# A decoder layer on one core: the causal mask moves from a bf16 product on TensorE to a GpSimd select on the copied scores

## The reference, cut to what matters

```python
# B = 8 sequences of S = 512 rows, D = 512, H = 16 heads of 32
x = x + self_attention(layernorm(x))            # q and k normalised per head
x = x + cross_attention(layernorm(x), ctx)      # only the 32 largest scores of a row count
x = x + ffn(layernorm(x))                       # quantised 512 -> 2048 -> 512

# in self_attention:
scores = jnp.einsum('bhqd,bhkd->bhqk', q, k) * scale
causal = jnp.tril(jnp.ones((s, s), dtype=bool))
scores = jnp.where(causal, scores, mask_value)
attn = jax.nn.softmax(scores, axis=-1)
```

## Time and profile before

| what | value |
|---|---|
| median of 3 runs | 3978.51 us (3974.26 to 3980.03) |
| the profiled execution | 3970.88 us, its span 3968.7 us |
| busy: PE, DVE | 3343.2 us (84%), 3333.4 us (84%) |
| busy: ACT, POOL | 2460.3 us (62%), 1789.4 us (45%) |
| chain that ended last, by engine | DVE 42%, PE 26%, issue 10%, POOL 10%, ACT 4% |

### The profile page before, as it was taken

One profiled execution on the slowest core, in us unless ns is written; L12 is line 12 of the kernel. 1 busy time (PEld: TensorE's weight loads), 2 busy tenths in 40 slices (PEclk: granted clock), 3 DMA queues, 4 the chain that ended last, 5 costly groups with the idle time before them and its releaser, 6 DMA issues.

```text
span 3968.7 us, 61337 instructions
## 1 busy us (share of the span) xinstructions
PE 3343.2 (84%) x18502; PEld 2462.5 (62%) x18502; DVE 3333.4 (84%) x7699; ACT 2460.3 (62%) x4921; POOL 1789.4 (45%) x2316
## 2 busy tenths in 40 slices
PE   2487799998999889998999898998899888877765
PEld 1365577766666676666666666666666666555542
DVE  4312299999999999999988999999989999999962
ACT  3344467666766677666766676667766676555533
POOL 0123234445544454545654555446544554344433
PEclk7778878888989988988988898998898898887767
DMA  8122322232222222322323222222232221211100
GB/s 276 49 54 58 102 72 70 81 83 72 69 67 82 62 63 74 91 78 62 85 73 83 66 68 70 77 66 64 78 94 78 62 70 41 62 46 35 33 22 19
DMA packets 167443, 283.04 MB, mean 71 GB/s; under 512 B 40639, under 2 KB 52939, under 8 KB 166606
## 3 DMA queue, kind: packets, MB, share of 16 engines
q1 hardware_dynamic: 160782, 275.98, 25.5%
q10 hardware_dynamic: 6336, 3.15, 0.3%
HBM read 113.27 MB, written 31.46 MB: 36 GB/s over the span
## 4 chain that ended last, share of the span: by engine, by line
DVE 42%; PE 26%; issue 10%; POOL 10%; ACT 4%; SPq 3%; DMA 1%; DVEq 0%; POOLq 0%; ACTq 0%
DVE cW L881 18%; DVE top L876 14%; PE bank L682 6%; PE bank L607 5%; PE bank L654 4%; SPq L513 3%; POOL srs L1147 3%; PE bank L593 2%; DVE smx L1017 2%; PE bank L670 2%; DVE hh L966 2%; PE bank L635 2%; POOL cS L1168 1%; DVE hmx L969 1%; POOL hh L1115 1%
## 5 line engine op out<-in xcount | busy, mean ns | idle before, releaser
L881 DVE MATCH_REPLACE8 cW<-top,cW 128x512 f32<-128x512 f32 x1536 | 1026.5, 676 | 0.0
L876 DVE MAX8 top<-cW 128x8 f32<-128x512 f32 x1536 | 981.0, 680 | 0.0
L1168 POOL TENSOR_TENSOR cS<-cS,cW 128x512 f32<-128x512 f32 x512 | 663.1, 1317 | 216.0 <-ACT cW L825 216.0
L797 ACT ACTIVATE PT<-bank 128x512 f32<-128x512 f32 (+3 forms) x1024 | 537.6, 525 | 359.1 <-PE bank L593 355.0
L607 PE MATMUL bank<-cv,PT 128*128 128x33 f32 x4096 | 600.0, 294 | 126.0 <-ACT PT L797 125.3
L607 PEld LDWEIGHTS bank<-cv,PT 128*128 128x128 f32 x4096 | 569.9, 214 | 161.9 <-ACT PT L797 155.4
L1175 POOL TENSOR_SCALAR cnb<-top 128x2 f32<-128x2 f32 x256 | 49.1, 192 | 894.1 <-DVE top L876 880.7
L607 PEld LDWEIGHTS bank<-sv,PT 128*128 128x128 f32 x2560 | 403.9, 213 | 77.7 <-ACT PT L797 54.2
L593 PE MATMUL bank<-ident,cS 128*128 128x128 f32 x2048 | 355.2, 302 | 73.4 <-POOL cS L1168 73.4
L825 ACT ACTIVATE cW<-cW,cnb 128x512 f32<-128x512 f32 x512 | 347.8, 733 | 107.9 <-DVE cW L881 107.4
L682 PE MATMUL bank<-w_group,xT 128*128 128x384 f32 x1024 | 406.3, 545 | 0.0
(11 more groups left out here) (151 smaller groups left out, 6087.0 us busy)
## 6 DMA issues: line engine op xcount, KB each, us to landing
sk_stack<-part SPq DMA_DIRECT2D x512, 64.0 KB, 2.0
sq_stack<-part SPq DMA_DIRECT2D x512, 64.0 KB, 2.0
ck_stack<-part SPq DMA_DIRECT2D x512, 64.0 KB, 2.0
cq_stack<-part SPq DMA_DIRECT2D x512, 64.0 KB, 2.0
w_group<-wa_by_group SPq DMA_DIRECT2D x32, 768.0 KB, 4.6
w_group<-wc_by_group SPq DMA_DIRECT2D x32, 768.0 KB, 4.3
feed<-in_x SPq DMA_DIRECT2D x32, 256.0 KB, 3.0
feed<-in_ctx SPq DMA_DIRECT2D x32, 256.0 KB, 3.0
```

Of the source, the lines that this page charges most:

```text
L797: act.activation(PT[k][:, 0:n], turned_ps[k][:, 0:n], ACT.Copy).then_inc(turned_read, step("turned_read", label))
L876: dve.max(top8[:, j, r, :], src[:]).then_inc(topk, step("topk", (c, r, "max", j)))
L881: dve.match_replace(cW[j][:], top8[:, j, r, :], src[:], REPLACED).then_inc(topk, step("topk", (c, r, "replace", j)))
L1168: pool.tensor_tensor(cS[m % 2][j][:], cS[m % 2][j][:], cW[j][:], ALU.subtract).then_inc(cprob, step("cprob", (m, j)))
```

## The change

The bf16 product is gone, with its two constants. In its place POOL has one `affine_select` for each pair of heads, on the diagonal blocks of both heads in `sP`, which writes -1e30 where the key is behind the query. DVE's maxima wait for a new semaphore `masked` in place of ACT's copy, and the select waits for ACT's copy of the pair's second head. In POOL's queue `causal_mask(s, 0)` stands behind `inner_quant`, `causal_mask(s, 1)` behind `rows_ln` and ahead of `x1_ln`.

```diff
@@ scores (PE)
-                                      start=True, stop=False)
-                            pe.matmul(ps[:, qt * P:(qt + 1) * P], ident16[:], mask16[:], start=False,
-                                      stop=True).then_inc(score_full, step("score_full", label))
+                                      start=True, stop=True).then_inc(score_full, step("score_full", label))
@@ self_maxima (DVE)
-                            dve.wait_ge(score_read, upto("score_read", ("self", s, 2 * half + 1)))
+                            dve.wait_ge(masked, upto("masked", (s, half)))
@@ POOL
+                    def causal_mask(s, half):
+                        if on(s):
+                            pool.wait_ge(score_read, upto("score_read", ("self", s, 2 * half + 1)))
+                            diagonal = sP[half][:, :, (s % NT) * P:(s % NT + 1) * P]
+                            pool.affine_select(out=diagonal, in_=diagonal, compare_op=ALU.is_ge, fill=MASKED, base=0,
+                                               pattern=[[0, 2], [-1, P]], channel_multiplier=1).then_inc(
+                                                   masked, step("masked", (s, half)))
...
                         inner_quant(s - 1)
+                        causal_mask(s, 0)
                         low_parts(now[3])
...
                         rows_ln(s)
+                        causal_mask(s, 1)
                         x1_ln(s)
@@ setup (POOL)
-                pool.memset(mask16[:], 0.0).then_inc(s_const, 1)
-                pool.affine_select(out=mask16[:], in_=mask16[:], compare_op=ALU.is_ge, fill=MASKED, base=0,
-                                   pattern=[[-1, P]], channel_multiplier=1).then_inc(s_const, 1)
-                pool.wait_ge(s_const, 3)
-                pool.tensor_copy(ident16[:], ident[:])
```

More of the change, by code:

```diff
@@ L43 @@
 SIGNALS = ["shared_full", "shared_read", "score_full", "score_read", "turned_full", "turned_read",
-           "smax", "sexp", "sbias", "cbias", "cexp", "topk", "so_full", "co_full", "recip", "so_norm", "co_norm",
+           "masked", "smax", "sexp", "sbias", "cbias", "cexp", "topk", "so_full", "co_full", "recip", "so_norm", "co_norm",
            "crest", "cprob", "sq_done", "rstd_done", "shat_done", "sumsq_done", "dve_rows", "pool_rows", "feed_stats",
@@ L214, in __init__ @@
             for p in range(2):
-                for name in ("smax", "sbias", "cbias"):
+                for name in ("masked", "smax", "sbias", "cbias"):
                     add(name, (n, p))
@@ L286, in decoder_layer @@
         ident = sb("ident", [P, P])
-        ident16 = sb("ident16", [P, P], BF16)
-        mask16 = sb("mask16", [P, P], BF16)
         ones16 = sb("ones16", [96, P], BF16)
@@ L301, in decoder_layer @@
         setup(nc, dict(W_attn=W_attn, b_attn=b_attn, wa_dram=wa_dram, wc_dram=wc_dram, banks=banks,
-                       ident=ident, ident16=ident16, mask16=mask16, ones16=ones16, bias16=bias16,
+                       ident=ident, ones16=ones16, bias16=bias16,
                        minus_half=minus_half, gcol=gcol, ccol=ccol, wscale=wscale, wproj=wproj, woT=woT, wgT=wgT, wuT=wuT,
@@ L368, in pipeline @@
             upto, step = C.upto, C.step
-            (shared_full, shared_read, score_full, score_read, turned_full, turned_read, smax, sexp, sbias, cbias,
+            (shared_full, shared_read, score_full, score_read, turned_full, turned_read, masked, smax, sexp, sbias, cbias,
              cexp, topk, so_full, co_full, recip, so_norm, co_norm, crest, cprob, sq_done, rstd_done, shat_done,
@@ L1227, in setup @@
     W_attn, b_attn, wa_dram, wc_dram = T["W_attn"], T["b_attn"], T["wa_dram"], T["wc_dram"]
-    banks, ident, ident16, mask16, ones16, bias16 = (T[k] for k in ("banks", "ident", "ident16", "mask16", "ones16", "bias16"))
+    banks, ident, ones16, bias16 = (T[k] for k in ("banks", "ident", "ones16", "bias16"))
     minus_half, gcol, wscale, wproj, woT = (T[k] for k in ("minus_half", "gcol", "wscale", "wproj", "woT"))
@@ L1289, in _ @@
                 pool.memset(ident[:], 0.0).then_inc(s_const, 1)
-                pool.memset(mask16[:], 0.0).then_inc(s_const, 1)
                 pool.memset(ones16[:], 1.0)
                 pool.memset(minus_half[:], -0.5)
-                pool.wait_ge(s_const, 2)
+                pool.wait_ge(s_const, 1)
                 pool.affine_select(out=ident[:], in_=ident[:], compare_op=ALU.not_equal, fill=1.0, base=0,
                                    pattern=[[-1, P]], channel_multiplier=1).then_inc(s_const, 1)
-                pool.affine_select(out=mask16[:], in_=mask16[:], compare_op=ALU.is_ge, fill=MASKED, base=0,
-                                   pattern=[[-1, P]], channel_multiplier=1).then_inc(s_const, 1)
-                pool.wait_ge(s_const, 3)
-                pool.tensor_copy(ident16[:], ident[:])
             @block.vector
@@ L1336, in _ @@
             def _(pe):
-                pe.wait_ge(s_const, 3)
+                pe.wait_ge(s_const, 2)
                 for k in range(4):
```

## The result

The changed kernel takes 4001.25 us, the median of 5 runs (3995.27 to 4005.89), against 3978.51 us for the kernel before: a ratio of 1.005, 95% interval 1.0039 to 1.0062, or +23 us. Its profiled execution took 3997.8 us.

A forecast was written before the change was run, and what follows sets the result against it. DVE was taken to bound the full pipeline, PE close behind, and a ring the filling stage. The terms 9.6 + 14.4 + 3 + 11 - 6 = +32 us gave 4010 us, 0.8% slower; 8-in-10 range 3985 to 4038 us.

The forecast's parts named there:

- eight slots like 74: Half 1 of eight head-norm slots: select behind the second subtraction, DVE's maxima 1.2 us later each, 9.6 us in all.
- six slots like 70: Half 1, select also behind the rows' layer norm: DVE stands 6.2 us, recovers 3.8; net 2.4 each, 14.4 us.
- six slots like 66: Half 1 of six slots: DVE loses 1.2 us, swallowed by its 2.27 us wait for the output projection: 0.
- the x1 chain: Six slots: select ahead of the x1 rows' layer norm, on the way to the output projection: 0.5 us each, 3 us.
- filling stage: Slots 2, 6, 10, 14, 18: bias 1.6 us and squares 1.2 us later, less 0.7 for PE; 11 us for five groups.
- TensorE: PE's starts 0.07 us closer per dropped mask, seen only where PE sets the pace: 6 us gained over seven sequences.
- Rival (a): A select is much dearer than its columns say, up to 1.25 us: +31 more, 4041 us; 12%.
- The tight first halves: Half 0 of slots 39, 55, ...: 0.73 us between POOL and DVE against 0.6 needed; no cost at 0.4 us of select.
- the three waits behind the stall: After slot 70's maxima: DVE's waits of 0.94 and 0.47 us for subtractions, 2.42 us for the SiLU, would vanish: 3.8 us.
- (b): Stalls are swallowed in the eight slots and the filling stage: within 8 us of before, about 3984 us; 15%.
- (c): PE, not DVE, sets the pace over more of the pipeline, so the kernel gets faster: 3956 us; 7%.
- (d): POOL's added reads collide with DVE's two-input product, up to 0.4 us at each of 128: 4061 us at most; 4%.

The follow-up runs named there:

- the two complementary runs: Changed kernel with the product instead of the select in half 1 of head-norm slots: 3981.89 us; and select only there, product elsewhere: 4011.04 us.
- the early place: Changed kernel with the select ahead of the subtractions in head-norm slots: 3997.86 us; the same with the select only from slot 20: 3986.82 us.
- the complement: Changed kernel with the select only in half 1 of the slots s modulo 4 = 2 and the product in the other 224 halves: 4011.04 us.

## Why the prediction was right

The forecast (slower, by stalls of DVE behind POOL's queue) holds. The time came out 9 us under it, inside the range. That the sum came so near is partly luck, since two of its terms were too small in opposite directions. Its steps, with the trace of the changed kernel against that of before, whose spans are 27 us apart (the medians 23):

| term | predicted | in the trace |
|---|---|---|
| eight slots like 74 | 8 x 1.2 = 9.6 | 8 x 1.0 = 8 |
| six slots like 70 | 6 x 2.4 = 14.4 | 6 x 3.3 = 20 |
| six slots like 66 | 0 | 1.0 each, 0.6 to 1.0 given back |
| the x1 chain | 6 x 0.5 = 3 | 6 x 0.4 = 2 |
| filling stage | 11 | 14 (the times say 11) |
| TensorE | -6 | -17, the remainder |

**The select's price**, 0.40 us from one block's 0.29 and the slope of a one-input operation, measured 0.416. Rival (a), a dear select, is out. **The slots like 74**: the mechanism is shown by the two complementary runs and by the early place, which has no stall there, and the size is that of the gap, 0.92 us: the hand-overs of 0.1 us each were a little too large (select to maxima is 0.03 us in slot 74: 1951.65 + 0.42 to 1952.10). **The slots like 66** were swallowed as argued. **The tight first halves** cost nothing.

**The slots like 70.** The step "they now start at 1826.84: DVE stands for 6.2 us ... Net 6.2 - 3.8 = 2.4 us" was right in its form, the three waits behind the stall are gone, but two sizes were off. DVE recovers 4.8 us and not 3.8: beside the three waits L962 ran in 1.06 us and not in the 1.75 of the earlier trace rows, which is 0.7 us of it. And the stall is 5.9 us where POOL's head norm is on time, as I had assumed everywhere, so 1.2 us net (slot 86 of the complement), and 7.3 us where PE's clock was low ahead of it, 3.3 us net. The second case was in none of my steps. It is all six slots in the changed kernel, 12.8 of the 20 us; the stalls that I had priced make 7.3 us, half of my 14.4.

**The filling stage.** The times give 11 us (+23 with all selects, +12 with the product in that stage), as predicted; the trace's 14 hold 3.5 us between the maxima of slots 3 and 4 that a run with the program of before has as well. The two parts of the step are there: the bias's 1.5 us in slot 2, and for the squares 1.15 us net in slots 5 and 13, with 1.2 predicted. The "- 0.7 for PE" per group is neither shown nor refuted: with the product gone the maxima of slot 21 come 326.5 us behind the first ones in one trace and, with the product in three slots of each sequence, 324.2 us in another, against 325.8 before, and programs that are the same there differ by up to 4.6 us.

**TensorE** is the term whose size failed: "12 x 0.07 = 0.8 us per sequence, 6 us over seven sequences". The starts moved by 0.08 us as read, but the stretches in which PE sets the pace give back 1.5 us per sequence (0.2, 0.6 and 0.7 us in slots modulo 16 = 15, 0 and 8), some 9 us, and slots 62 and 94 another 3.7 us each. In slot 62 it is the clock again, the window of the changed kernel:

```profile
1570.00:1583.00 13.00, 11.85 (x74) 9.57 (x73) 12.83 (x33) 8.33 (x19) 8.38 (x12) 0.85 0.23 81
```

In the same stretch of the trace of before, 1547 to 1560 us, the granted clock is 0.64. That the product's removal caused that is not shown: slots 78 and 110 of the same traces don't have it. Taken alone the removal brought only 6 us, since the clock of the slots like 70 took 11.8 back (five of six, 1.9 to 3.3 us each). On top of the selects it brought 17: there three of the six had the low clock already with the product kept, and the removal added three (6.4 us). That is some 5 us of the 11 between the two. In the traces another large difference lies in slots modulo 16 = 14 and 15, with the wait for the output projection: against before, five such places lose 8.9 us with select and product and gain 7.4 in the changed kernel, which is 16 us for the removal, but they gain only 1.2 with the product alone gone. Why is open; single executions scatter by nearly as much. The Trainium skill ("Trainium Kernel Development and Optimization", Performance Expectations) says that matmul busy time is a poor measure of how near a kernel is to roofline, because matmuls are pipelined. The runs agree: a group of 124.9 us went, for 6 us alone and 17 us beside the selects, and PE's busy time fell by 46.3 us only.

**Rivals.** (b), swallowed stalls, is out: the late selects alone cost 31 us. (Its sum was wrong as well: 14.4 + 3 - 6 on the median is 3990 us, not 3984.) (c), PE over more of the pipeline, is out as a whole (-6 us alone), but what there was of it I had put too low. (d), collisions of POOL's reads with DVE's product L966, is out as a cost: in the changed kernel 11 of the 128 products have a select beside them, these took 0.81 us in the mean, and all products together 116.4 us against 118.0 before. What a collision there was fell on the select. Four of the 256 took 0.85 to 0.87 us and not 0.41; each had begun while the product ran, as here:

```profile
1101.68 0.87 DVE L962 TENSOR_TENSOR hh<-hh,uc 128x512 f32<-128x512 f32 x1
1101.94 0.87 POOL L1185 TENSOR_SCALAR_AFFINE_SELECT sP<-sP 128x256 f32<-128x256 f32 x1
```

**What stays open.** The early place should have gained 13 us by its stalls and gained 2 to 6, in two kernels. In the trace of the first, 10 us are in slot 62 and in the drain; in that of the second, 9.3 us are in the slots modulo 16 = 14, in all five sequences. In the first these slots go both ways (two of the five are shorter), so it is not shown that the later subtractions delay the output projection there. Nor is it shown what puts PE ahead by 1.3 us at slot 70 in the complement, whose products are all there. No version was faster than the kernel before with the mask in it.

## What to carry to other kernels

Work that is moved to a half idle engine costs what its place in that engine's queue costs, not its busy time: 31 of 256 selects, each of 0.42 us, made nearly the whole loss, and the others were about level with what they replaced. Read for each moved instruction when its engine is done with what stands ahead of it and when the waiting engine comes; a stall found that way is to be set against the waits behind it that it swallows, and taking the stall away brings these back. When an engine that is not the bound gets less to do, ask how long it will then wait. And before a difference of a few microseconds between two traces is put down to an edit, look at a stretch that the edit leaves alone: here such a stretch differed by up to 4.6 us.

## What the hardware did that I had not expected

In slot 70 TensorE, earlier by 1.3 to 1.5 us, waited 2.8 to 3.05 us instead of 1.5 for the same input, its granted clock over the next 6 us was 0.72 instead of 1.00 (0.50, the level of 1.2 GHz, in a part of it), and the chain behind it, up to POOL's head norm, came 2.1 us later. Over 72 cases the late chain went with the lower clock every time (53 with, 19 without). With the wait it went nearly always: all 12 waits up to 1.53 us left the chain on time, and 51 of 53 from 1.88 us up did not. That the longer wait makes the clock fall is the likely reading and not shown by an experiment: the run that was to take TensorE's lead away in these slots did not do so. The clock can also fall in one execution and not in another with the same program ahead of it, as at 256 us.
